# Moving accumulator set-up to ScalarE, and the own terms of two attention sums into VectorE's loop

## What is computed

```python
# layer L1_gnn, twice (H = 4 heads of 64 columns); edges are given, plus one loop edge per node
h = (x @ W).reshape(n_nodes, Hh, Cc)
a_src = (h * att_src).sum(-1)
a_dst = (h * att_dst).sum(-1)
alpha = leaky_relu(a_src[src] + a_dst[dst])
m = jax.ops.segment_max(alpha, dst, num_segments=n_nodes)
e = jnp.exp(alpha - m[dst])
denom = jax.ops.segment_sum(e, dst, num_segments=n_nodes)
w = e / jnp.clip(denom, 1e-16)[dst]
out = jax.ops.segment_sum(w[:, :, None] * h[src], dst, num_segments=n_nodes)
```

## Time and profile before

| | us |
|---|---|
| median of 3 runs | 6087.88 |
| lowest and highest | 6084.16, 6088.64 |
| the profiled execution, its own time | 6083.15 |
| its span, first to last instruction | 6081.4 |
| mean granted TensorE clock | 0.81 of full |

### The profile page before, as it was taken

The page is one execution under the profiler, slowest core; times in us unless marked ns, Lnnn a source line. Parts: engine busy times, 40 slices in busy tenths (PEclk is TensorE's granted clock), DMA queues, the critical chain, the costliest instruction groups (busy, mean ns, idle before and its releaser), DMA issues. The chain is left out here.

```text
span 6081.4 us, 104839 instructions
## 1 busy us (share of the span) xinstructions
PE 4472.6 (74%) x20716; PEld 3480.6 (57%) x20717; DVE 3415.5 (56%) x11843; ACT 2378.3 (39%) x8232; POOL 3578.9 (59%) x3704
## 2 busy tenths in 40 slices
PE   5967675867877787676777788886956566665996
PEld 1444443756666666554555688885744444444885
DVE  5888885236655666646988544444265555556012
ACT  3745541227998899523555211111210010001221
POOL 3767740756775777363777277773447757772221
PEclk6989985988888888688999755556977887786998
DMA  4023322123443344333333111122143333332555
GB/s 80 1 66 103 104 78 83 55 86 99 106 106 94 102 107 106 89 103 116 103 103 99 27 8 8 8 8 62 61 124 105 105 93 103 105 105 94 189 186 189
DMA packets 295811, 542.46 MB, mean 89 GB/s; under 512 B 85287, under 2 KB 179153, under 8 KB 295324
## 3 DMA queue, kind: packets, MB, share of 16 engines
q0 software_dynamic: 162656, 381.68, 24.2%
q1 hardware_dynamic: 119942, 146.53, 7.5%
q10 hardware_dynamic: 13110, 13.08, 0.6%
HBM read 474.76 MB, written 66.28 MB: 89 GB/s over the span
## 5 line engine op out<-in xcount | busy, mean ns | idle before, releaser
L1475 PE MATMUL psM<-G,S 128*128 x3328 | 1073.6, 443 | 476.5 <-SPq L1379 325.9
L1439 POOL DMA_INDIRECT G<-table_ones,ids x1176 | 1123.0, 955 | 508.4 <-issue 353.4
L1475 PEld LDWEIGHTS psM<-G,S 128*128 128x128 f32 x3328 | 666.9, 219 | 715.3 <-issue 613.8
L1533 DVE TENSOR_TENSOR XN<-XN,psM 128x257 f32 (+1 forms) x1680 | 701.1, 417 | 542.5 <-PE psM L1475 522.6
L1211 POOL DMA_INDIRECT G<-table_gat,ids x840 | 810.9, 965 | 265.9 <-issue 255.3
L1261 PE MATMUL psM<-G,S 128*128 128x260 f32 (+1 forms) x2752 | 785.8, 438 | 233.0 <-ACT G L1184 213.2
L1261 PEld LDWEIGHTS psM<-G,S 128*128 128x128 f32 x2752 | 625.1, 275 | 355.5 <-issue 188.1
L1184 ACT ACTIVATE G<-G 128x64 f32<-128x64 f32 x3360 | 824.7, 333 | 6.8
L1211 POOL DMA_INDIRECT G<-table_ffn_gat,ids x548 | 522.2, 953 | 176.6 <-issue 166.7
L1279 DVE TENSOR_TENSOR acc<-acc,psM 128x260 f32 (+1 forms) x1388 | 450.7, 325 | 270.0 <-DVE acc L1279 133.4
L1458 PE MATMUL psV<-Ot,Pk 128*128 128x272 f16 (+1 forms) x2496 | 485.0, 304 | 88.2 <-ACT Pk L1401 73.8
(11 more groups left out here) (486 smaller groups left out, 7438.4 us busy)
## 6 DMA issues: line engine op xcount, KB each, us to landing
w1s<-in_L_ffn_W SPq DMA_DIRECT2D x32, 1024.0 KB, 8.8
w2s<-in_L_ffn_W SPq DMA_DIRECT2D x32, 1024.0 KB, 6.0
land<-out_by_choice SPq DMA_DIRECT2D x75, 256.0 KB, 3.5
G<-table_ones,ids POOLq DMA_INDIRECT x1176, 2.8
G<-table_gat,ids POOLq DMA_INDIRECT x840, 2.8
rows_by_token<-XN SPq DMA_DIRECT2D x20, 640.0 KB, 3.3
G<-table_ffn_gat,ids POOLq DMA_INDIRECT x548, 2.4
table_ones<-XN SPq DMA_DIRECT2D x10, 640.0 KB, 6.5
```

The lines of the kernel that those rows point to most:

```text
L1439: pool.indirect_dma_start(G[:, k % RG * EG + j, :], None, table, bass.IndirectOffsetOnAxis(ids[:, k % GB, j:j + 1], 0)).then_inc(gathered[ ...
L1475: nc.tensor.matmul(psM[:, j, 0:W], S[:, g, j, :], G[:, bass.ds(at[g * EG + j], 1), :].rearrange("p a w -> p (a w)"), start=True, stop=True ...
L1533: nc.vector.tensor_tensor(ab, ab, psM[:, n0 % EG, 0:W], ALU.add).then_inc(added, 1)
```

## The change

1. ScalarE no longer waits for `cleared` before the first indices, in both kinds of sum.
2. ScalarE sets up the accumulators of the four wide sums that need it, and of "gat1" and "gat2", behind its first `take_ids`; it zeroes with `activation(..., Copy)` from a column of zeros (`before[:, 0:1]`), 25 row tiles at once.
3. In "gat1" and "gat2" the own terms leave the set-up. VectorE adds those of one row tile at groups 0 and 4 of a trip, that is once per 16 tiles: a multiply of 256 columns into `own_rows`, an add of 4 columns to the denominator, a wait, an add of 256 columns into `acc`, a wait. So that the 26th such place is left out, the last trip is written out behind the loop. "gatf" keeps its own terms in the set-up.

```diff
+                if own is not None:
+                    own_rows = sb("own_rows", [P, HEADS * c])
...
-                        act.wait_ge(cleared, 1)
                         for k in range(DEEP - 1):
                             take_ids(None, k)
+                        if own is not None:
+                            nc.scalar.activation(acc[:, :, 0:W], before[:, 0:1].unsqueeze(1).to_broadcast([P, NT, W]), ACT.Copy).then_inc(added, EG)
...
+                        def add_own(i, g):
+                            t, n = bass.ds(i * 2 + g // GB, 1), i * 2 + g // GB
+                            dve.wait_ge(added, i * TRIP + (g * EG + EG))
+                            nc.vector.tensor_tensor(own_rows[:, :].rearrange("p (h c) -> p h c", h=HEADS),
+                                                    XN[:, t, 0:HEADS * c].rearrange("p a (h c) -> p (a h) c", h=HEADS),
+                                                    own[:, t, :].rearrange("p a h -> p (a h)").unsqueeze(2).to_broadcast([P, HEADS, c]), ALU.mult).then_inc(own_step, 1)
+                            den = acc[:, t, HEADS * c:HEADS * c + HEADS].rearrange("p a h -> p (a h)")
+                            nc.vector.tensor_tensor(den, den, own[:, t, :].rearrange("p a h -> p (a h)"), ALU.add).then_inc(own_step, 1)
+                            dve.wait_ge(own_step, n * 3 + 2)
+                            ab = acc[:, t, 0:HEADS * c].rearrange("p a d -> p (a d)")
+                            nc.vector.tensor_tensor(ab, ab, own_rows[:, :], ALU.add).then_inc(own_step, 1)
+                            dve.wait_ge(own_step, n * 3 + 3)
...
-                        begin().then_inc(added, EG)
+                        if own is None:
+                            begin().then_inc(added, EG)
                         score(None, 0)
-                        with dve.Fori(0, trips) as i:
+                        def trip(i):
...
+                                    if own is not None and not (isinstance(i, int) and i * 2 + g // GB >= NT):
+                                        add_own(i, g)
...
+                        with dve.Fori(0, trips - 1) as i:
+                            trip(i)
+                        trip(trips - 1)
...
-                        act.wait_ge(cleared, 1)
                         for k in range(AHEAD):
                             take_ids(None, k)
+                        if begin is not None:
+                            begin(added)
...
-            def from_one():
-                nc.vector.memset(acc[:, :, 0:D], 0.0)
-                return nc.vector.memset(acc[:, :, D:D + 1], 1.0)
+            def from_one(set_up):
+                nc.scalar.activation(acc[:, :, 0:D], before[:, 0:1].unsqueeze(1).to_broadcast([P, NT, D]), ACT.Copy).then_inc(set_up, EG - 1)
+                nc.scalar.activation(acc[:, :, D:D + 1], ones[:, 0:NT].unsqueeze(2), ACT.Copy).then_inc(set_up, 1)
...
-            edge_sum("gat1", LB, tabg[0], WGAT, acc, self_terms(XN, own, acc, 64), AD, 64)
+            edge_sum("gat1", LB, tabg[0], WGAT, acc, None, AD, 64, own=own)
```

More of the change, by code:

```diff
@@ L1128, in _, with edge_sum @@
                             nc.vector.tensor_tensor(zo[:, :, :], zo[:, :, :], att.AD[:, :, HEADS:2 * HEADS], ALU.subtract).then_inc(scored, 1)
-        def edge_sum(name, e, table, W, acc, begin, AD, c, each=None):
+        def edge_sum(name, e, table, W, acc, begin, AD, c, own=None, each=None):
             with ExitStack() as ctx:
@@ L1155, in edge_sum @@
                                                                        sem("scored"), sem("powered"), sem("weighed"))
-                z_step = sem("z_step")
+                z_step, own_step = sem("z_step"), sem("own_step")
+                if own is not None:
+                    own_rows = sb("own_rows", [P, HEADS * c])
                 TRIP = DEEP * EG
@@ L1541, in _ @@
                                 make_s(None, k, j)
-                        begun = begin()
-                        if begun is None:
+                        if begin is None:
                             dve.sem_inc(added, EG)
-                        else:
-                            begun.then_inc(added, EG)
                         if job is not None:
@@ L2132, in add_to @@
             return nc.vector.tensor_tensor(v, v, w, ALU.add)
-        def zeros_in(acc, W):
-            return lambda: nc.vector.memset(acc[:, :, 0:W], 0.0)
         def self_terms(TB, own, acc, c):
@@ L2214, in program @@
                   tables=[(tabg[0], XN, WGAT, "kept")], att=att)
-            edge_sum("gat1", LB, tabg[0], WGAT, acc, self_terms(XN, own, acc, 64), AD, 64)
+            edge_sum("gat1", LB, tabg[0], WGAT, acc, None, AD, 64, own=own)
             dense("gat2", FIVES, acc_row, ln=False, fold=denominators, front=divided, col=column["gat1"], W=(wgt["gat2"], WGAT + HEADS),
                   into=table_row, tables=[(tabg[1], XN, WGAT, "kept")], att=att)
-            edge_sum("gat2", LB, tabg[1], WGAT, acc, self_terms(XN, own, acc, 64), AD, 64,
+            edge_sum("gat2", LB, tabg[1], WGAT, acc, None, AD, 64, own=own,
                      each=lambda i: add_to(tile_of(X, i), row["gat2"][:, :]))
@@ L2232, in program @@
             dense("gcn", SHORT_END, xn_row, got=True, W=(wgt["gcn"], D), by=wgt["gcn1"], scale=DINV, into=xn_row, tables=[(tabx, XN, D, "kept")])
-            tile_sum("gcn", LA, tabx, D, XN, lambda: None,
+            tile_sum("gcn", LA, tabx, D, XN, None,
                      job=Job(LF, LF.by_pool, list_dram[LF.name][0:LF.slots, :]), each=lambda i: add_to(tile_of(X, i), row["gcn2"][:, :]))
@@ L2297, in zeros_beside, with begin @@
             def zeros_beside(acc, W):
-                def begin():
-                    nc.vector.memset(TR[:, NT, :], 0.0)
-                    return nc.vector.memset(acc[:, :, 0:W], 0.0)
+                def begin(set_up):
+                    nc.scalar.activation(TR[:, NT, :], before[:, 0:1].to_broadcast([P, D]), ACT.Copy).then_inc(set_up, EG - 1)
+                    nc.scalar.activation(acc[:, :, 0:W], before[:, 0:1].unsqueeze(1).to_broadcast([P, NT, W]), ACT.Copy).then_inc(set_up, 1)
                 return begin
@@ L2319, in program @@
                   W=(wgt["sage2"][:, :, D:2 * D], D), into=xn_row, hold=turned_rows, tables=[(tab1[2], XN, D, "kept")])
-            tile_sum("sage2", LB, tab1[2], W1TAB, acc, zeros_in(acc, W1TAB), each=own_into_x,
+            tile_sum("sage2", LB, tab1[2], W1TAB, acc, zeros_beside(acc, W1TAB), each=own_into_x,
                      later=(turned_rows, wgt["sage2"][:, :, 0:D]))
```

## The result

| | before | after |
|---|---|---|
| median of 7 runs each, us | 6088.64 | 6111.70 |
| lowest and highest, us | 6084.16, 6090.54 | 6104.31, 6116.45 |
| ratio, 95% interval | | 1.0036 [1.0026, 1.0046] |
| the profiled execution, us | 6083.15 | 6113.43 |

A forecast was written before the change was run, and what follows sets the result against it. POOL's gathers set the pace: its start, 1.25 us per gather, plus its stalls. 9.4 - 0.6 + 13.2 - 5.0 = 17.0 us off the 6087.88 median gives 6070.9 us, range 6062 to 6082.

The forecast's parts named there:

- the last trip written out: In "gat1" and "gat2": same work in straight code, without loads of loop registers, so no effect on the time.
- the 22.0 of gains in the sum: All sums: earlier indices 9.4 us, less 0.6 for first gathers, plus 13.2 from the long gathers of "gat1" and "gat2".
- Rival B: "gat1" and "gat2": own step too long for VectorE, lag grows, POOL waits for indices; 28 us slower, 6116; chance 0.07.
- The early indices: Start of all seven sums: ScalarE copies indices at block entry, POOL's first gather starts 0.61 to 1.61 us earlier; 9.4 us.
- C: Starts of the sums: early indices don't start POOL early, something else at block entry holds it; 6079.7 us; chance 0.09.
- First gathers beside the selection matrices: Starts of sums: POOL's first gathers, now beside DVE's 12 selection matrices, lose 0.1 us per stage, 0.6 in all.
- The long gathers: Starts of "gat1" and "gat2": without DVE's wide multiplies, gathers of 7.45 and 7.66 us become plain; 13.2 us won.
- D: Starts of "gat1" and "gat2": the long gather has another cause than DVE's multiplies and stays; 6081 us; chance 0.04.
- the zeroing: Set-up of sums: ScalarE's zeroing, at most 5.8 us, hides beside POOL's gathers and doesn't delay the first score; no effect.
- Own terms against gathers: Loops of "gat1" and "gat2": DVE's own adds lengthen gathers by 0.1 us at each of 50 steps, 5 us (0 to 21).
- A: Loops of "gat1" and "gat2": each of 50 own steps may hold a gather 0.3 to 0.42 us; 6083.9 us; chance 0.12.
- Own-step lag without a hole: Loops of "gat1" and "gat2": own steps of 1.4 to 1.8 us don't make ScalarE's lag grow; 0, up to 3 us.

The follow-up runs named there:

- grown: Kernel before the change, with 20 empty VectorE instructions added to each trip of the "gat2" loop (trip of 279, no own terms in it); ratio 1.0009.
- gat1only: Changed kernel with the own terms of "gat2" back in its set-up, the rest of the change kept; ratio 0.9967 to the kernel before.
- starts: Changed kernel with the own terms of "gat1" and "gat2" back in the set-up; ratio 0.996 to the kernel before, 0.9991 in a second comparison.
- placed: Changed kernel with 32 already satisfied waits ahead of the "gat2" loop on VectorE, moving it by 16 instructions; ratio 0.9975 to the kernel before.

## Why the prediction was wrong

- **The failed step** is the sentence that the last trip written out, and with it the own terms in the loop, cost only their work: "the same work in straight code", "one answer, nothing". I priced instructions by what they do and never asked where they lie. The 19 more per trip, and what now stands ahead of the loop (the last trip of "gat1", some 170 instructions, among it), put its end beyond what the engine holds. Neither of the two does it alone: the longer trip at the old place ("grown") and the old length at the new place ("gat1only") have no hole. In the place of "nothing" the runs showed a hole of 3.4 to 3.75 us at eleven branches of "gat2", whose trips took 44.4 us where they took 40.2, 46 us in all against the 22.0 of gains in the sum. The length of the trips (255 and 259 before, beside the block of 256 cited above) would have made it a rival.
- **Rival B had the path of the loss, and its 6116 us near the measured 6111.70 is luck.** Right was: VectorE late, ScalarE hands out indices late, POOL waits. Wrong was what starts it: B lost 1.0 us at each of 50 own steps in both sums by the adds' own length; measured are none in "gat1" and 4.2 us per trip in "gat2", set off by the fetch, with an own step of 1.4 us. B's price doesn't hold together either: by its 7.3 us from score to exponential an own step may take 2.2 us, by its 1.0 us lost out of 2.5 only 1.5. I gave it 0.07.
- **The early indices: right.** First gather after the start of the block: 1.0 us in "gat1", "gat2", "sage1", "sage2" where it was 2.6, and 1.0 in "gatf" where it was 1.6. C did not happen.
- **First gathers beside the selection matrices: mis-sized.** The first two took 1.65 and 1.03 us in "gat1" and 1.50 and 1.04 in "gat2", and over 0.945 each they are 0.6 to 0.8 us in six of the sums, not 0.1. Over seven sums that is some 4.3 us instead of 0.6; by the same count the old order had some 1.5 already. The matrices are not the reason by themselves: "gatf" has twelve of them there too, and its first two took 0.98 and 0.99. There the memset of `G` is over before the first gather; in the six others the long first gather starts inside it. But a gather inside the memset of "sage1" took 0.94, so the reason stays open. The last gathers of the five other sums come 1.1 to 1.9 us earlier, 7.3 us in all; of that 5.0 arrives at their last adds. In "gatf" the last gather comes 1.6 us earlier and the last add 1.0 later, which I can't explain from one trace each.
- **The long gathers: right.** Gone in both sums, and D, by the inference of the Trainium skill that the prediction quotes (SBUF — State Buffer, "Who interferes with whom"), with them: with the wide multiplies moved, the 7.45 us became 1.03. In "starts", where they are back, so is a gather of 7.3 us, and in "gat1only" "gat2", with its multiplies, has one of 7.5 and "gat1" has none. The first score did come with the landing of the first four gathers, 8.4 us into the block (forecast 7.95), and not behind the zeroing (5.62 us, forecast 5.5 to 5.8), which three plain sums and the two attention sums have.
- **Own terms against gathers: right in kind, over-sized.** One that hits, in "gat2":

```profile
1974.45 0.42 DVE L1288 TENSOR_TENSOR own_rows<-XN,own 128x256 f32 x1 [1.50 <-issue]
1974.50 1.19 POOL L1214 DMA_INDIRECT G<-table_gat,ids  x1 [0.30 <-issue]
```

  It starts 0.05 us ahead of the gather, as in the earlier trace rows, and the gather takes the same 1.19 us and ends 0.82 us behind it. But most miss. All gathers of "gat1" together are 2.8 us over 0.945 each, of which 0.8 in the first two; before it was 2.0 beside the long one. So nothing in "gat1" and 2.9 us in "gat2", where I had 5.0 for both. A did not happen.
- **Own-step lag without a hole: right in "gat1", zero; not measured in "gat2" on the first chip,** where the bias stands beside it. The own step took 1.4 us, as in the sum. "gat1" kept its 40 us per trip and ended 7.4 us earlier; the sum gave 5.5 for it (1.6 + 6.5 - 0.1 - 2.5).

Shown: whether the hole is there depends on where a loop of given length lies, packets of code come with it each time, and without it the changed kernel is 30 us faster on one of the other chips. By its trace it is 3.3 of the 4.2 us by which the trips of "gat2" are longer on the first chip. Not shown: the other 0.9 us, the whole time without the hole on the first chip, and the exact edge. The offset of a loop in the code can't be read from a trace; the 238 above is worked out from where the hole came and went and from the second hole of "placed".

## What to carry to other kernels

Count the instructions of a loop's trip on each engine, before an edit and after. The Trainium skill gives the block that is fetched as 256 instructions (Runtime: NRT & Kernel Launch, "Instruction fetch mechanics"); the trips with a hole here had 278 and 279, those of 255 never had one, and trips of 259 to 279 ran without one as well. Whether such a trip pays some 3.5 us at each branch back depended on where the code ahead of it ended, so that 32 instructions ahead of the loop turned the hole off and 178 turned it on; either keep the trip below the block or look at the branches back after every edit. In a profile the signs are idle time ended by "issue" at the top of a trip, once per trip, and packets on an instruction queue inside the loop.

And what a hole costs depends on the slack around it. With engines that run level with the one that sets the pace (here POOL, 40 us per trip) a trip became longer by more than the hole, 4.2 us for 3.3; on the other chips eleven holes cost the changed kernel 30 us, and the kernel before, with twelve holes and the waits ahead of them, was 14 us longer.

## What the runs showed of the hardware

- From a branch back to the first instruction of the next trip VectorE takes 0.2 to 0.3 us, and in the loops that fetch 3.4 to 3.75 us on the first chip (2.7 to 4.1 over all such runs), with five packets of 8 KB per trip on q14, two of them within the hole.
- Empty instructions (`engine_nop`) have no one price on VectorE: 64 in a row moved the first add from 12.3 to 25.9 us (0.21 us each), 256 moved it to 49.3 (0.14 each), and ten in the loop took 0.25 to 0.3 us together (0.03 each). Of the semaphore waits that already hold, 64 (32 instructions) moved it from 12.3 to 12.9.
- A gather issued by POOL that starts during VectorE's wide multiplies of two SBUF operands ends 0.81 to 0.83 us behind them: 7.45 and 7.66 us, and 7.3 to 7.5 where they were put back, beside 1.03 and 1.04 without them.
- Chips of the same kind run this program in 6088 or in 7424 to 7550 us, and the same change is worth 0.36% on one and nothing on the other.
